# Half of the index searches of a routed FFN moved from ahead of it to among its up products

## The reference

```
h = xf @ W_router + b_router                 # 4096 x 32, xf: t normalised
G_ek, idx_ek = top_k(softmax(h).T, k=128)    # each of 32 experts takes 128 tokens
tokens = xf[idx_ek]
up  = tokens @ W_up[group] + b_up            # 8 groups of 4 experts, 341 wide
Eout = silu(up) @ W_down[expert] + b_down
y = zeros.at[idx_ek].add(G_ek * Eout)        # a token may be taken by several experts
out = t + y
```

## Time and profile before

| what | value |
|---|---|
| median of 3 runs | 203.8 us (203.35 to 204.65) |
| the profiled execution | 202.58 us, span 200.3 us |
| PE busy | 128.4 us (64%) |
| POOL busy | 108.4 us (54%) |
| DVE busy | 99.3 us (50%) |
| ACT busy | 81.0 us (40%) |

### The profile page before, as it was taken

The page is one execution under the profiler, slowest core; times in us unless marked ns, Lnnn a source line. Parts: engine busy times, 40 slices in busy tenths (PEclk is TensorE's granted clock), DMA queues, the critical chain, the costliest instruction groups (busy, mean ns, idle before and its releaser), DMA issues.

```text
span 200.3 us, 2418 instructions
## 1 busy us (share of the span) xinstructions
PE 128.4 (64%) x670; PEld 83.7 (42%) x673; DVE 99.3 (50%) x409; ACT 81.0 (40%) x290; POOL 108.4 (54%) x121
## 2 busy tenths in 40 slices
PE   1999965304116341110126899999999659999992
PEld 1558954201005110000003666666777524444592
DVE  2464998974774882102001021194674962973600
ACT  3265999346992772110134455534334000000062
POOL 2028479986351377777744366866878678300000
PEclk9999999855555555555555699999999969999999
DMA  4999999999755252222220113333424334599167
GB/s 108 298 341 302 292 289 201 305 398 264 190 157 159 88 211 70 63 65 67 65 56 19 49 15 38 29 27 27 40 26 39 29 28 38 101 324 382 63 183 236
DMA packets 33710, 28.45 MB, mean 142 GB/s; under 512 B 6848, under 2 KB 27408, under 8 KB 33568
## 3 DMA queue, kind: packets, MB, share of 16 engines
q1 hardware_dynamic: 26785, 21.70, 37.5%
q0 software_dynamic: 5472, 4.48, 15.3%
q10 hardware_dynamic: 1440, 2.13, 3.3%
HBM read 17.61 MB, written 10.68 MB: 141 GB/s over the span
## 4 chain that ended last, share of the span: by engine, by line
PE 48%; DVE 17%; POOL 12%; issue 10%; another core or an unknown queue 9%; DMA 2%; ACT 1%; SPq 0%; POOLq 0%; DVEq 0%
PE PZ L1184 7%; PE PT L1148 7%; PE PM L1148 6%; PE PZ L1162 6%; POOL rs L472 4%; PE PM L1184 3%; PE PT L1184 3%; PE PM L1162 3%; POOL rs L465 3%; PE PT L992 2%; DVE wdn L935 2%; DVE junk L923 2%; PE PT L1137 2%; POOL act L478 2%
## 5 line engine op out<-in xcount | busy, mean ns | idle before, releaser
L511 POOL DMA_INDIRECT acc<-X,idx x27 | 42.0, 1557 | 18.4 <-DVE X L967 8.0
L502 POOL DMA_INDIRECT xg<-token_rows,idx x32 | 30.4, 949 | 16.3 <-DVE idx L920 8.3
L935 DVE TENSOR_SCALAR_CACHE_REDUCE wdn<-wide,slot_token 128x1024 bf16<-128x1024 f16 x20 | 25.0, 1272 | 5.5 <-PE PZ L1184 5.5
L1125 PE MATMUL PZ<-cum,onehot 32*128 32x129 f16 x32 | 6.7, 265 | 31.3 <-DVE idx L920 18.8
L1040 PE MATMUL PZ<-stage_w,X 128*128 128x192 f32 x64 | 14.7, 381 | 6.9 <-DVE act L767 6.5
L1162 PE MATMUL PZ<-wdn,act 128*128 128x128 f32 x132 | 17.4, 277 | 1.1 <-DVE X L967 1.1
L645 ACT ACTIVATE X<-PZ 128x512 f32<-128x512 f32 x4 | 2.4, 597 | 38.3 <-PE PZ L1189 38.3
L1125 PEld LDWEIGHTS PZ<-cum,onehot 32*128 32x128 f16 x32 | 3.0, 99 | 34.9 <-issue 30.8
L1162 PEld LDWEIGHTS PZ<-wdn,act 128*128 128x128 f32 x132 | 16.0, 191 | 2.1 <-DVE X L967 1.4
L967 DVE TENSOR_SCALAR X<-PZ,xg 128x128 f32<-128x128 f32 x22 | 7.6, 349 | 18.6 <-PE PZ L1162 18.6
L620 ACT ACTIVATE junk_a<-PZ,slot_half 128x128 f16<-128x128 f32 x16 | 5.8, 363 | 26.7 <-issue 20.8
(11 more groups left out here) (180 smaller groups left out, 278.3 us busy)
## 6 DMA issues: line engine op xcount, KB each, us to landing
X<-in_x SPq DMA_DIRECT2D x8, 256.0 KB, 5.2
acc<-zero SPq DMA_DIRECT2D x4, 512.0 KB, 6.3
acc<-x SPq DMA_DIRECT2D x8, 256.0 KB, 5.3
token_rows<-xf SPq DMA_DIRECT2D x8, 256.0 KB, 2.3
xf<-acc ACTq DMA_DIRECT2D x8, 256.0 KB, 5.7
x<-acc SPq DMA_DIRECT2D x8, 256.0 KB, 7.4
out<-X SPq DMA_DIRECT2D x8, 256.0 KB, 2.5
wup<-in_L_ffn_W_up SPq DMA_DIRECT2D x1, 1364.0 KB, 7.8
```

What stands on the lines that cost most here:

```text
L502: nc.gpsimd.indirect_dma_start(out=xg[:, e, :], out_offset=None, in_=rows[:, :], in_offset=bass.IndirectOffsetOnAxis(ap=idx[:, e:e + 1], a ...
L511: nc.gpsimd.indirect_dma_start(out=acc[i][:, :], out_offset=bass.IndirectOffsetOnAxis(ap=idx[:, e:e + 1], axis=0), in_=eo[:, e, :], in_off ...
L935: nc.vector.tensor_scalar(hot(k)[:, r], columns[:, r], slot_token[:, k:k + 1], None, ALU.is_equal, ALU.add, accum_out=found_in[:, k * HOT_ ...
L1125: mm(find_bank(e), onehot[r, g, :], cum[r, g, 0:P + 1], start=True, stop=True).then_inc(s_find, 1)
```

## The change

The finds of experts 0 to 15 stay where they were, ahead of the FFN. Those of experts 16 to 31 go, four at a time, into up(1) to up(4): a find stands before each of the three up products and the fourth behind them. DVE works the four `token_number` of the next unit just before it scales the first expert of a unit, for unit 0 (experts 16 to 19), 1 (20 to 23), 2 (24 to 27) and 3 (28 to 31). DVE counts all of these itself; ACT counts only the odd ones of the first sixteen. The moved finds have two PSUM banks instead of four, the other two belonging to the down products. `slot_token`, which needs all indices, is made at expert 10 instead of ahead of the FFN.

```
+FIRST_FINDS = 16
 def on_act(e):
-    return e % 2 == 1
+    return e < FIRST_FINDS and e % 2 == 1
+def finds_by_unit(k):
+    lo = FIRST_FINDS + PER * (k - 1)
+    return range(lo, lo + PER) if 1 <= k and lo < E else ()
...
         def find_bank(e):
+            if e >= FIRST_FINDS:
+                return PZ[:, e % 2, 0:P + 1]
             return PZ[:, (e + 2) % 4, 0:P + 1]
...
+            for e in range(FIRST_FINDS):
+                token_number(e)
             for e in range(E):
-                token_number(e)
-            v.wait_ge(s_idx, E)
-            link(nc.vector.tensor_scalar(slot_token[:, :], idx[:, SCATTERED:E], -float(TOK // 2), None, ALU.add))
-            for e in range(E):
+                if e == UNITS[UNIT_OF[e]][0]:
+                    for f in finds_by_unit(UNIT_OF[e] + 1):
+                        token_number(f)
                 if e == HOT_AFTER[0]:
+                    v.wait_ge(s_idx, E)
+                    link(nc.vector.tensor_scalar(slot_token[:, :], idx[:, SCATTERED:E], -float(TOK // 2), None, ALU.add))
                     v.wait_ge(s_col, 16)
...
             def find(e):
-                if e >= 4:
+                if e >= FIRST_FINDS:
+                    pe.wait_ge(s_idx, e - 1)
+                elif e >= 4:
                     pe.wait_ge(s_idx, e - 3)
...
-            for e in range(E):
+            for e in range(FIRST_FINDS):
                 find(e)
...
             def up(k):
                 pe.wait_ge(s_gTs, k + 1)
+                finds = list(finds_by_unit(k))
                 for j, (f0, fn) in enumerate(FF):
                     at = 3 * k + j
+                    if finds:
+                        find(finds.pop(0))
                     if at >= 2:
                         pe.wait_ge(s_act, at - 1)
                     mm(dst, wup[...], xgT[...], start=True, stop=True).then_inc(s_up, 1)
+                for e in finds:
+                    find(e)
...
             def down(k):
                 if k == 0:
-                    pe.wait_ge(s_idx, E)
+                    pe.wait_ge(s_idx, FIRST_FINDS)
```

## The result

The changed kernel took **197.85 us** (median of 5, 196.37 to 199.61) against 203.53 us (202.17 to 204.65) before: ratio 0.972 [0.964, 0.979]. Three later sets gave 0.966 [0.959, 0.973] (with the column load moved, e3), 0.978 [0.968, 0.988] (e10) and 0.970 [0.963, 0.977] (e12). The sign and the range of the prediction held; of the 13.8 us forecast (203.8 to 190) only 5.7 came.

A forecast was written before the change was run, and what follows sets the result against it. Bound: late DVE updates hold up the searches, hence the FFN and POOL's gathers and scatters. Gains of 10.3 (scatters) and 5.4 (slack) less 1.7 (clock) give 14.0 us: 190 us instead of 203.8; own range 187 to 193, whole range 187 to 212.

The forecast's parts named there:

- FFN start: First up product on PE, after ACT's last count: at 75.5 instead of 105.89, so 30.4 us earlier.
- Finds in the up products: Sixteen finds moved between PE's products: 1 us per unit, 4 us; up(4) at 98.8, last index at about 102.
- DVE instead of ACT: Eight counts move from ACT to DVE, 3 us of DVE beside PE's FFN, harmless unless links are late.
- the disputed price: Cost of a DVE link while gathers stream: between 0.02 and 2.94 us; the lower bound taken for the point.
- rival 1: Late updates stay while gathers stream and the FFN stands behind them: midway 211 us, slower; chance 0.36.
- rival 2: The same lateness but milder, links late by 0.5 to 1.7 us: 190 to 204, about 197 us; chance 0.13.
- T: Time when the last index is there; span = T + 79.5, and the change breaks even at T = 120.8.
- Gathers: POOL's 32nd gather goes out at 107.2 instead of 111.15, if index 31 is there by 106.9.
- Scatters: POOL's first scatter at 108.4, then one every 2.01 us, last at 160.7, 10.3 us earlier than 171.02.
- The end: Sums start at 173.1, PE waits for them: slack of 5.4 us gained, 1.7 us lost to half clock in the transposes.
- the guess: DVE's lateness came behind a burst of 36 DVE updates within seven microseconds; spaced later indices would thus be prompt.
- The 0.14: Chance said to lie outside the range of 187 to 212 us, which takes in somewhat over half of rival 1.

The follow-up runs named there:

- e3: The changed kernel with the load of the one-hot columns issued after the first scaled expert: 198.13 us, ratio 0.966.
- e10: The changed kernel, unchanged, run again on another chip beside the kernel before: 196.95 us, ratio 0.978.
- e12: The changed kernel, unchanged, run again on the chip of e11: 199.0 us, ratio 0.970.
- e5: The changed kernel with one scatter behind every two gathers from the eighteenth gather on, on the chip where the kernel before took 187.78 us: 186.5 us, 0.991.
- e1: The kernel before, with POOL's first gather waiting for the last index: 212.77 us, ratio 1.046.
- e14: The kernel before with a POOL fill of 64x640 behind each gather, on the chip of e11: 209.6 us, ratio 1.029.
- e16: The changed kernel with the smallest POOL fill (64x32) behind each gather: 196.3 us, ratio 0.962.
- e15: The kernel before with the smallest POOL fill (64x32) behind each gather, one gather per 1.37 us: 202.95 us, ratio 0.989.
- e11: The kernel before, unchanged, run again on another chip: 205.5 us, beside a median of 203.53 us of eleven runs there.
- e18: The kernel of e13 with a 64x256 POOL fill behind ten of the first fourteen gathers: 190.5 us, ratio 0.941 to the kernel before.
- e13: The kernel of e5 (changed kernel, one scatter behind every two gathers from the eighteenth on) on the chip of e11: 191.7 us, 0.942 to the kernel before.
- e17: The kernel of e13 with the smallest POOL fill (64x32) behind the first seventeen gathers: 192.0 us, ratio 0.941 to the kernel before.
- e8: The changed kernel with eight searches ahead of the FFN instead of sixteen, on the chip of e5: 195.9 us.

## Why the prediction had the sign and missed the size

*FFN start, 75.5.* Right: 75.25.

*Finds in the up products.* Right where updates are prompt (e5: unit 4 at 95.8, forecast 98.8, last index 100.1, forecast 102). Here units 2 and 4 came 13 and 15 us later than in e5, and the last index was there at 115.3.

*DVE instead of ACT, and the disputed price.* This is **the step that failed**. It asked what a link of DVE costs among the up products, and took the lower bound because the sixteen would be spaced. The links are indeed prompt. But the price was not the links' to pay: with the FFN beside the stream, PE's completions are the ones held up, and ACT, DVE's count and PE's next product all hang on them. The rows in front of L925 showed a victim, and I priced the victim. Rivals 1 and 2 had the right effect (late updates go on while gathers stream) at the wrong instruction; the measured time lies in rival 2's 190 to 204 and at its 197, with T at 115.3, inside its 107 to 121. Chance given: 0.13. That the sign held is thus in part luck: the last index came 13 us after the 102 of the forecast, and the change would have broken even at 120.8.

*Gathers, 107.2.* The last went out at 116.09: 8.9 us, the core of the miss: the 13.3 us of the last index less the slack of some 5 us. Two causes add up. PE stood 7.41 us for one late update and shorter for others, and half a clock behind it took 2.07 instead of 1.12 us for each of two pairs, 1.9 us.

*Scatters, 2.01 each, last at 160.7.* (172.01 - 117.34) / 26 = 2.10: 2.4 us more. The 2.01 was read from the last four scatters before; over all twenty-six steps they took 2.12 there and 2.07 in e10. *The end.* From the last scatter to the sums 11.2 instead of 12.4, from the sums to the end 14.25 instead of 13.2 (the first sixteen transposes took 3.78 us, against 1.95 at full clock). Sum of the deviations: 8.9 + 2.4 - 1.2 + 1.1 = 11.2, which is 197.5 - 186.3. The structure (PE done, waiting for the sums behind POOL's queue, half the clock in the transposes) was right.

*The reason given for the guess*, the burst of 36 updates, is refuted by e1: the burst alone delays nothing, and PE's updates are late at 104 and 129 us, when it is over for more than 20 us. What the change escapes is not a burst but a dependence: before, 32 searches stood in the stream and the FFN behind them; now half of them do, and the FFN takes the rest of the damage.

*The chances.* The 0.14 said to lie outside the range doesn't fit its own terms: with 0.05 of it below 187, it leaves 0.09 above 212, a quarter of rival 1's 0.36, while the text puts nearly half of rival 1 there.

*Is the gain real?* Where it was measured, beside a kernel before of 203.5 to 203.8 us (the first set, e10, e12, and e3 with the columns moved), yes: 2 to 3%, with intervals from 1 to 4%. Of six chips on record five are of this kind by the time of the kernel before. On the sixth my sum (186.3) would stand against a kernel before that is there already: 187.78 us with spans of 184.5 to 187.5, and e5, whose POOL queue has the same length of work, ends at 185.5. From these I estimate a ratio of about 1.0 there; it is not measured.

Open: what in the chip holds the updates back, and why one chip doesn't. The trace records no queue for it. The fills slow the issuing of gathers and their traffic together, so which of the two does it is open too. No row read here shows an update of ACT or POOL known late; why is not explained.

The Trainium skill, "Advanced Engine Details and Errata" (DMA Bandwidth Details), puts an increment at about one cycle. The changed kernel's link takes 0.04 us (84.55 to 84.59) in all, which leaves room for that without measuring it; the ten waits of 2.94 us in the earlier trace rows don't agree. The skill's page "VectorE: DVE Perf Modes" (The TRN2 errata) warns that increments at a high rate can deadlock another engine and advises to space them. The prediction read that as a rule on waits, which the page doesn't state, and no run here shows a deadlock. For these waits it was the gathers that had to be spaced: e1 is dense and prompt without them, e14 prompt with them slowed.

## What to carry over

Where an instruction waits for microseconds with "remote" as its releaser, ask first what else streams at that time, and price the lateness for every engine that completes work beside the stream, not for the one that shows it. Slow the suspected stream and look at the same rows (20.3 us of waits became 0.3): that separates cause from victim in one run. And before a gain of 3% is believed, see the kernel before on more than one chip: here the two kinds of chip differ by 8%.

## Hardware behaviour not expected

- Gathers (128 rows each, software queue) every 1.253 us delay completion updates of PE and DVE: 2.94 us a wait before the change, and in e1 a product was known 20.3 us after its end. At 1.37 us one silu waited 12.31 us (e16), and 9.8 us remain before the index (e15) where e11, on another chip, had 20.3; at 1.87 us 0.3 us remain (e14). With ten gathers at 1.55 us the longest wait for "remote" is 1.09 us (e18).
- It builds up: from the stream's start some 6 us pass until DVE's updates are late in the kernel before, some 12 until PE's are in the changed one. What has built up outlasts the stream, by 7.8 us in e1, and goes with a pause of POOL: no such wait is left after 3.27 us before 96.29 and after 5.02 in e13, one of 1.64 us after the 3.25 of the kernel before. After such a pause scatters and gathers in turn don't bring it back (e13); without one, late updates go on beside them until 102.8, with one more at 128.33 (e17).
- By the time of one and the same program, five chips are of this kind and one isn't: 203.5 and 187.8 us. Profiles show the late updates on four of the five, and their absence on the one in e5 to e8.
